# Attention's weights prepared in seven pieces between the last scans instead of in one block

## What is computed

```
# scan
x_dbl = x @ W_xproj.T;  delta = softplus(x_dbl[..., :64] @ W_dt.T + b_dt)
dA = exp(delta[..., None] * A)                 # A: 256 x 16
dBx = (delta * x)[..., None] * B[:, :, None, :]
h = dA_t * h + dBx_t;  y = einsum('bdn,bn->bd', h, C_t)
x = layernorm(x + y)
# cross attention
Q = layernorm(x @ Wq.T);  K = layernorm(ctx @ Wk.T);  V = ctx @ Wv.T
x = layernorm(x + softmax(Q K^T / 4) V @ Wo.T)
# experts
x = layernorm(x + experts(x))
```

## Time and profile before

| | |
|---|---|
| median of 3 runs | 1261.09 us (1260.95 to 1265.19) |
| the profiled execution's own time | 1260.9 us |
| its span | 1259.1 us |
| mean granted clock of PE | 0.924 of full speed |
| busy over the span: PE, DVE, ACT, POOL | 81%, 70%, 62%, 63% |

### The profile page before, as it was taken

How to read it: one execution, slowest core, us unless ns; L and a number is a source line. 1 busy time by engine, 2 the same in 40 slices (tenths; PEclk the granted TensorE clock), 3 DMA queues, 4 the chain that set the end, 5 groups by cost and what they waited for, 6 DMA issues and landing times. The chain is left out here.

```text
span 1259.1 us, 28796 instructions
## 1 busy us (share of the span) xinstructions
PE 1013.6 (81%) x9883; PEld 857.3 (68%) x9883; DVE 886.3 (70%) x1717; ACT 783.3 (62%) x1771; POOL 796.8 (63%) x736
## 2 busy tenths in 40 slices
PE   6888888888884788888888861259999999999960
PEld 4776777777763566666666640159989989999960
DVE  4999999999995577777777756755555555555434
ACT  6999999999991466666666632135555555555424
POOL 2999999999995477777777744051346346346342
PEclk8999999999996899999999975579999999999995
DMA  5243333233231011111111002041344344343227
GB/s 171 97 124 125 102 120 124 94 127 124 91 93 40 14 40 38 38 38 38 38 42 42 31 28 75 0 139 51 64 118 99 68 114 97 71 110 62 29 30 271
DMA packets 62947, 101.20 MB, mean 80 GB/s; under 512 B 10433, under 2 KB 36642, under 8 KB 60834
## 3 DMA queue, kind: packets, MB, share of 16 engines
q1 hardware_dynamic: 50594, 83.31, 20.0%
q0 software_dynamic: 12288, 17.05, 8.2%
HBM read 78.93 MB, written 21.40 MB: 80 GB/s over the span
## 5 line engine op out<-in xcount | busy, mean ns | idle before, releaser
L584 POOL TENSOR_TENSOR scan_hc<-scan_state,scan_c_sb 128x1024 f32<-128x1024 f32 x128 | 299.9, 2371 | 18.4 <-DVE scan_state L470 16.4
L470 DVE TENSOR_TENSOR_SCAN scan_state<-scan_decay,scan_drive_ps 128x512 f32<-128x512 f32 x256 | 295.5, 1201 | 7.6 <-issue 2.6
L1648 POOL DMA_INDIRECT acc<-expert_rows,input_lst x64 | 113.3, 1771 | 178.9 <-DVE expert_rows L1777 163.6
L297 PE MATMUL scan_drive_ps<-all_ident,scan_scaled 128*128 128x128 f32 x1024 | 169.6, 291 | 57.1 <-DVE scan_state L470 44.5
L1751 DVE TENSOR_TENSOR expert_hid_lo<-expert_hid,expert_hid_hi 128x512 fp32r<-128x512 f32 x128 | 88.5, 691 | 171.3 <-ACT expert_hid_hi L1735 160.2
L1730 ACT ACTIVATE expert_hid<-expert_h_ps,expert_b 128x512 f32<-128x512 f32 x128 | 88.1, 688 | 188.6 <-PE expert_h_ps L618 172.7
L297 PEld LDWEIGHTS scan_drive_ps<-all_ident,scan_scaled 128*128 128x128 f32 x1024 | 119.7, 146 | 98.4 <-DVE scan_state L470 75.9
L387 ACT ACTIVATE scan_decay<-scan_delta,scan_a_neg 128x508 f32<-128x508 f32 x256 | 167.4, 712 | 18.9 <-DVE scan_state L470 18.0
L308 PE MATMUL scan_y_ps<-all_ident,scan_hc 128*128 128x128 f32 x1024 | 158.8, 280 | 3.3 <-POOL scan_hc L584 3.3
L397 ACT ACTIVATE scan_scaled<-scan_dxT,scan_bT 128x256 f32<-128x256 f32 x352 | 149.4, 499 | 0.3 <-DVE scan_dxT L488 0.3
L616 PE MATMUL expert_o_ps<-weights_w_hi,expert_hid_hi 128*128 128x256 f32 x512 | 143.2, 280 | 2.1 <-issue 2.1
(11 more groups left out here) (213 smaller groups left out, 2324.1 us busy)
## 6 DMA issues: line engine op xcount, KB each, us to landing
scan_c_sb<-rows SPq DMA_DIRECT2D x128, 256.0 KB, 3.1
weights_w<-w SPq DMA_DIRECT2D x16, 1024.0 KB
table<-all_row SPq DMA_DIRECT2D x32, 132.0 KB, 1.8
scan_xT<-xT SPq DMA_DIRECT2D x8, 512.0 KB, 4.4
scan_x_tok<-x_tok SPq DMA_DIRECT2D x8, 512.0 KB, 5.1
attn_ctxT<-ctxT SPq DMA_DIRECT2D x32, 128.0 KB, 2.5
acc<-all_row SPq DMA_DIRECT2D x32, 128.0 KB, 1.7
final_a<-acc SPq DMA_DIRECT2D x8, 512.0 KB, 7.1
```

The source lines that it names most:

```text
L297: last = pe.transpose(drive_ps[k][:, j * P:(j + 1) * P], scaled[:, p.slot, j, k * P:(k + 1) * P], ident[0][:])
L470: dve.tensor_tensor_scan(state[:, p.slot, k, :], decay[:, p.slot, k, :, :].rearrange("p b t -> p (b t)"), drive_ps[k][:], 0.0, ALU.mult, A ...
L584: pool.tensor_tensor(hc[:, p.slot, :, :], state[:, p.slot, :, :], c_sb[:, p.slot, :].unsqueeze(1).broadcast_to([P, KH, GT]), ALU.mult).the ...
L1648: pool.indirect_dma_start(out=acc_dram, out_offset=bass.IndirectOffsetOnAxis(ap=lst[h.parity][:, n:n + 1], axis=0), in_=rows[h.part][:, t, ...
```

## The change

`prepare` is split into three functions that are called from DVE's `group` for the last group alone: after step 8 the cast of w_q, after step 9 that of w_kv, after step 10 that of w_o, after step 11 the small constants, and after steps 12, 13 and 14 the three remainders. The same instructions with the same shapes are issued, none is added or left out. The block before the last statistics is gone.

```diff
+                        if grp.final and n in (8, 9, 10):
+                            attention.round_weights(dve, n - 8)
+                        if grp.final and n == 11:
+                            dve.wait_ge(const_loaded, 16 * consts)
+                            attention.small_constants(dve, ident[0])
+                        if grp.final and n in (12, 13, 14):
+                            attention.rest_of_weights(dve, n - 12)
...
                 groups(dve, group)
-                dve.wait_ge(const_loaded, 16 * consts)
-                attention.prepare(dve, ident[0])
                 for half in range(2):
                     statistics(Group(GROUPS // 2 - 1, 1), half)
...
+    def round_weights(self, dve, n):
+        if n == 0:
+            dve.wait_ge(self.loaded, self.count)
+        dve.tensor_copy(self.w_parts[n][0][:], self.w[n][:]).then_inc(self.w_high, 1)
+
+    def rest_of_weights(self, dve, n):
+        hi, lo = self.w_parts[n]
+        dve.wait_ge(self.w_high, n + 1)
+        dve.tensor_tensor(lo[:], self.w[n][:], hi[:].bitcast(F32), ALU.subtract).then_inc(self.ready, 1)
```

More of the change, by code:

```diff
@@ L1171, in load, with small_constants @@
             sp.dma_start(sbuf[:], dram).then_inc(self.loaded, 16)
[L1173 to L1177, removed]
+    def round_weights(self, dve, n):
[6 more added lines that the diff above has]
+        dve.tensor_tensor(lo[:], self.w[n][:], hi[:].bitcast(F32), ALU.subtract).then_inc(self.ready, 1)
+    def small_constants(self, dve, ident):
         for i in range(2):
@@ L1182, in prepare @@
         dve.tensor_copy(self.ident_bf[:], ident[:]).then_inc(self.ready, 1)
-        for n, (w, (hi, lo)) in enumerate(zip(self.w, self.w_parts)):
-            dve.wait_ge(self.w_high, n + 1)
-            dve.tensor_tensor(lo[:], w[:], hi[:].bitcast(F32), ALU.subtract).then_inc(self.ready, 1)
 class ChoiceConstants:
```

## The result

| | before | after |
|---|---|---|
| median of 8 runs each, us | 1260.88 (1259.83 to 1265.19) | 1265.60 (1263.66 to 1268.26) |
| ratio, 95% interval | | 1.0033 (1.002 to 1.0047) |
| profiled execution, us | 1260.9 | 1264.13 |
| its span, us | 1259.1 | 1262.3 |
| mean granted clock of TensorE | 0.924 | 0.924 |

The kernel became slower by 0.33%, some 4.2 to 4.7 us. The total was right. Its largest term was not, nor were three others, as the profile shows.

What follows compares the result with a forecast made beforehand. POOL's products, then the start of the last statistics, were taken to bound the end of the scan phase. 3.3 + 0.67 + 2.34 + 0.9 = 7.2 us, less 2.1, gave +5.1: 1266.2 us, range 1262.5 to 1271.5.

Steps and rivals of the forecast that it cites:

- largest term: After steps 9 and 10, the w_kv cast holds up DVE's scans and POOL runs dry before hc(10): +3.3 us so far.
- PE's clock: While DVE stands, PE stands too and slows to half speed; a slow step costs 0.54, two taken: +0.9 us.
- second rival: Every operation enters at POOL's next boundary, POOL pays only what the pieces hold: +2.2, 1263.3 us; chance 0.13.
- the first: Rival: DVE loses a close race to hc(11) after step 11, POOL then idles: +6.4 to +7.4 us; chance 0.35.
- near 397: Sign of the forecast: POOL's last product ends near 397 us in the profile after, instead of 389.62.
- The w_kv cast stands 6.8 us until POOL has nothing left: After step 9, step 10's scans wait behind the cast; hc(10) starts at 379.0 instead of 375.70 us: +3.3 so far.
- Small constants after step 11: DVE's scans end as hc(10) ends, DVE gets in first and POOL waits for the small constants: +0.67 us.
- The remainders at boundaries: After steps 12, 13, 14 each remainder enters at a POOL boundary and POOL waits: 0.60 + 1.14 + 0.60 = +2.34 us.
- The tail: Without the block, the last statistics start about 0.05 us behind PE's end instead of at 393.77 us: gain 2.1 us.
- All after it as before, only later: Sign of the forecast: everything behind the last statistics runs as before, only later; no term in the sum.
- The third: Rival: no conflict, the 5.62 us had another cause, the pieces hide in DVE's slack: -2.1, 1259.0 us; chance 0.05.

Runs made afterwards that it cites:

- before's first profile: The unchanged kernel before, the profile the forecast was read from: profiled execution 1260.9 us, first cast 5.62 us long.
- before's second profile: The kernel before profiled once more, unchanged: its one run took 1265.92 us, no ratio; first cast 0.89 us long.
- two scalings: The change with two scalings of twice the size in place of four, same values: ratio to before 1.002 (1.0006 to 1.0033).
- behind the moments: The change with the whole preparation put on DVE behind the last group's statistics and moments: ratio to before 1.0012 (0.9999 to 1.0024).
- on ScalarE: Casts, scalings and identity on ScalarE behind its last scaling, eps and remainders on DVE behind the moments: ratio to before 0.9993 (0.9978 to 1.0008).
- experiment 1: Both kernels profiled once more, unchanged: before took 1265.92 us, the change 1267.46 us, one run each.
- small constants kept in the block: The change, but small constants stay in front of the last statistics, casts and remainders spread: ratio to before 1.001 (0.9998 to 1.0021).

## Why the prediction was right, and where not

**The total.** +5.1 us was forecast, 4.7 us lie between the medians. That they agree is luck. The largest term rested on a wait that did not happen, PE's clock went the other way, one term was a quarter of what it measured, and one was missing; the errors cancel. By its own signs the forecast was wrong: it named casts of 0.4 to 2.3 us as the sign of the second rival and small constants above 2 us as that of the first, and the profile shows 1.22, 1.17 and 0.39 us and 6.58 us. POOL was not idle before hc(10), and ended its last product at 394.22 us where "near 397" had been written.

- *The w_kv cast stands 6.8 us until POOL has nothing left, +3.3.* This step failed. The cast took 1.17 us and entered at POOL's next boundary, and the three casts together moved hc(10) by 0.88. It rested on reading, one row of one execution, as a rule, that such a cast can't enter at a boundary between two ready POOL instructions. Ten other profiles show the opposite, one of before among them. POOL was starved all the same, but by the scalings.
- *Small constants after step 11, +0.67.* It was 2.54, as idle time of POOL before hc(12). I took four scalings as one piece of 0.60 us and asked only when the piece gets in. Each has to get in anew, and one POOL instruction passes between two of them.
- *The remainders at boundaries, +2.34.* Right: +2.35, with products 3.08 and 3.36 us from start to start (2.9 to 3.5 forecast).
- *PE's clock, +0.9.* Wrong in sign, by before's first profile. PE stood 6.77 us while the scalings stood, and ran at 0.50 of full speed from 380 to 384 us, but of that only 0.15 us reached DVE, ahead of a scan of step 13. At the end the higher clock gave back 0.88 us, and that was no term of the sum.
- *The tail, -2.1.* Right in kind: the statistics follow PE. Against before's second profile it is 3.21 to 1.19, -2.0. Against the first it is -2.96. The forecast kept 1.97 us for PE's last sums, and they took 1.09, at a granted clock of 1.00 instead of 0.50. In the kernels where they took 1.97 again (two scalings, behind the moments, on ScalarE) T is 2.06, as the forecast's 0.05 us behind PE would have it.
- *All after it as before, only later.* This was wrong, and was not in the sum at all: +1.4 us in the loop, from one DVE instruction fewer. The order of the operations was the same, and no row of before could price it.

By these the sum is 0.88 + 2.54 + 2.35 = 5.8, less 3.0, plus 1.4: 4.2 us.

**The rivals.** The first had the right place and the right kind, a stand at the small constants and POOL dry for up to 2.4 us before hc(12), for a reason of its own (a lost race), and a total that is too high since it stood on the 3.3. The second, each operation enters at POOL's next boundary, is the mechanism that every later run bears out; the rule of the Trainium skill named with experiment 1 holds in all of them, and only the 5.62 us of before's first profile stands against it. Its price of +2.2 left out that POOL goes first after each entry, and so that in a row of operations each but the first waits out one POOL instruction. With the 2.54 us that this costs, the casts at 0.88 and the tail at -2.96, the scan phase alone costs the +2.8 measured. The third is out: casts do stand behind POOL, and on ScalarE they don't.

## What to carry to other kernels

Slack of an engine is no cover for operations that wait for its neighbour, as DVE's casts, scalings and subtractions did for POOL's here: count them, not their work, for each waits out the neighbour's instruction in flight, and between two in a row one of its instructions passes. Put such pieces where the neighbour idles, merge them, move them to an engine that doesn't disturb it (ScalarE here), or keep a longer unrelated operation between them. And before a pause of several microseconds in one profile is taken for a rule, look at a second profile of the same kernel; the forecast's main term rested on a pause that the second profile didn't have. Where a change shifts the count of instructions, compare the loops behind it too, though nothing in them changed.

## What the runs showed of the hardware

- DVE's scaling of 2 elements a partition behind POOL's product of 1024 takes up to 2.39 us, and ends 0.03 us after the product. POOL's next instruction then goes ahead of DVE's next scaling, even back to back: 3 passed between four scalings (6.58 us), 1 between two (1.99).
- A subtraction of two SBUF operands also waits. With the small constants kept in the block one took 2.58 us instead of 0.67. POOL waits for it as well: scan_mean_std took 1.06 us instead of 0.20 beside one.
- The same eight matmuls of PE took 1.97 us at a granted clock of 0.50 and 1.09 at 1.00.
- One cast passed two boundaries (5.62 us). It happened in one profile of before and not in the other, and is unexplained.
- A loop that nobody touched ran 1.3 to 1.5 us slower in 25 passes when DVE had one or two instructions fewer ahead of it; with nine fewer (casts and constants on ScalarE) it did not. It comes with a stand of 0.38 us in the fourth pass and of some 0.12 us in every second pass after it that no semaphore ends. The runs tie it to the number of instructions: in four pairs of kernels the two differ by one. In the seven profiles with the stand a packet of instructions starts 0.55 to 0.84 us behind the fourth attn_res, in the others 0.66 to 2.00 us ahead of it. That the loading of code is the cause is argued only.
